# Weight splits inside other phases, decay factors at the start, the flag read in the last batch, and a landing buffer of its own

## The chip, the cores and the metric

The kernel runs on one core of a Trainium2 chip. The metric is the device time of one execution in microseconds (us); lower is better. Engines are called by their names in the profile: PE (TensorE matmul, with PEld its weight load), DVE (VectorE), ACT (ScalarE), POOL (GpSimd) and SP (SyncE, which here only issues DMAs; its queue is SPq).

## The reference

x has the shape 8 x 1024 x 256 (8 batches of 1024 tokens with 256 features). Four layers follow each other, each on the layernorm of x and added to x:

```python
x = x + attention(layernorm(x))          # 2 heads of 128, partial rope, causal softmax
x = x + ffn(layernorm(x))                # silu(x Wg) * (x Wu) @ Wd; int32 weights * 1/127, hidden 768
x = x + linear_attention(layernorm(x))   # 8 heads of 64, decay sigmoid(decay_log) per step, sigmoid gate
x = x + ffn(layernorm(x))                # the same weights again
```

The linear attention is a scan over the tokens: S = g S + k v^T, z = g z + k, out = (q S) / (q z + eps), with q and k being elu(.) + 1.

## The kernel before

x stays in SBUF as tensor X (64 tiles of 128 tokens x 256). Four phases run one after the other, each a block of five instruction streams that wait for each other by semaphores, with all engines meeting between phases: attention (8 batches), ff1, linear attention (8 batches in 16 halves of 512 tokens), ff2. A feed-forward phase works in 16 units of 512 tokens. To get precision from fp32r matmuls, an operand is split into a high part (a copy rounded to fp32r) and a low part (value minus high part), and two or three products are summed.

The feed-forward unit (lines 817 to 1071) is where most of what follows happens. In unit u each engine runs f = 0 to 5 over the hidden columns, 128 at a time, in this order:

- PE: gate(f) and up(f) (line 1026, 4 matmuls each), then down(f - 3) (line 1037, 16 matmuls). gate(f) waits for silu(f - 3), up(f) for h(f - 3), and down for both parts of h. The unit begins when both parts of its normalised, transposed input are there (pe_wait).
- ACT: silu(f) (L951), then the high part of h(f - 1) (L941). At f = 4, ahead of silu(4), it makes the high part of the input of unit u + 1 (act_high, L271), which waits for that input to have landed.
- DVE: h(f) (L990), then the low part of h(f - 1) (low_part, L974); in addition statistics of unit u + 2 at f = 0 and 1, the residual of unit u - 1 at f = 2 (L981), the normalisation of unit u + 2 at f = 3 (L156), and at f = 4 the 32 x 32 block transposes of unit u + 2 (dve_blocks, L255), which wait until the input of unit u + 1 has landed, as both pass through one buffer (ln_xn).
- POOL: 1/sqrt(var) for unit u + 2 (L167, L170), then the low part of the input of unit u + 1 (pool_low, L276).
- SP: 16 DMAs of 32 KB that put the transposed blocks of unit u + 1 in place (sp_move, L266). It waits for up(5) of unit u - 1, since the blocks land where that unit's low part lay (ln_xl, ff_odd_xl), and for the blocks.

The splits of weights stand where they are needed. The feed-forward weights (4608 columns of int32) are cast by POOL in the last attention batch (L465), their low part is taken in three pieces by DVE (L654) and squared in three pieces by ACT (L555) at steps 9, 10 and 11 of that batch; the sum says whether any low part is nonzero, and PE reads that flag (low_any) as a register at the begin of ff1 and ff2 and chooses between two and four products. At the begin of ff1 ACT copies the low weights (L933); at the begin of ff2 ACT casts the weights anew (L936) and DVE takes the low part (L968). At the begin of the linear phase ACT and DVE and POOL split its weights (L1225 to L1227, L1293, L1206, L1209), while decay factors are made from 12 columns by a chain DVE, ACT (Exp, Ln), DVE, ACT (Exp) (L1288 to L1303); PE waits for each part.

## Time and profile before

| what | before |
| --- | --- |
| median of 3 runs | 1981.17 us (1980.4 to 1982.3) |
| the profiled execution | 1982.85 us, its span 1981.1 us |
| PE busy | 1891.3 us (95%) |
| DVE busy | 1367.3 us (69%) |
| ACT busy | 889.7 us (45%) |
| POOL busy | 451.7 us (23%) |
| first matmul of attention, ff1, linear, ff2 | 13.72, 564.71, 853.80, 1698.05 us |
| ff1 units 1 to 14, ff2 units 1 to 14 | 244.48 us, 243.66 us |
| mean granted PE clock | 0.994 |

A timeline row gives the start in us from the span's begin, the duration in us, the engine, the line of the kernel, the instruction with its output and inputs and their shape, and in brackets how long the engine had been idle before it and who ended that. PE's matmuls overlap in these rows, so the distance of their starts is their pace. The granted clock is 1.00 at 2.4 GHz and 0.50 at 1.2 GHz.

### The profile page before, as it was taken

How to read it: one execution, taken by the hardware profiler on the slowest of the kernel's cores; microseconds unless marked ns; L12 is line 12 of the kernel's file. 1: busy time of each engine (PE TensorE's matmuls, PEld its weight loads, DVE VectorE, ACT ScalarE, POOL GpSimd, SP SyncE). 2: the span in 40 equal slices, each digit the busy share in tenths (PEclk: the TensorE clock that was granted, in tenths of full speed). 3: DMA queues.
4: the chain of work that ended last, by engine and by line, in shares of the span. 5: the costliest groups of instructions: out<-in, count | busy, mean ns of one | idle time of the engine just before them, and what ended most of it. 6: DMA issues, size and time to landing. Idle time of an engine off the chain costs nothing. (4 is left out here: it accounts for less than half of the span.)

```text
span 1981.1 us, 36996 instructions
## 1 busy us (share of the span) xinstructions
PE 1891.3 (95%) x12419; PEld 1639.4 (83%) x12419; DVE 1367.3 (69%) x3222; ACT 889.7 (45%) x1708; POOL 451.7 (23%) x362
## 2 busy tenths in 40 slices
PE   6999999999989999969999999999999998899998
PEld 5888888888778888858888888888888887788887
DVE  6666566656667888756766667766666677778885
ACT  5555556655654444453333333333333332444443
POOL 2112201220312222132222222222222222221220
PEclk9999999999999999989999999999999999999999
DMA  6100000000021111110000000000000000122222
GB/s 217 58 1 0 0 0 0 0 0 0 12 75 30 30 30 30 32 53 11 12 12 12 11 11 11 11 11 11 11 11 11 11 12 12 32 64 63 53 61 58
DMA packets 230887, 53.23 MB, mean 27 GB/s; under 512 B 209952, under 2 KB 229024, under 8 KB 230432
## 3 DMA queue, kind: packets, MB, share of 16 engines
q1 hardware_dynamic: 229696, 49.54, 11.7%
q10 hardware_dynamic: 1120, 2.75, 0.4%
q8 instruction: 43, 0.70, 0.2%
q14 instruction: 28, 0.23, 0.0%
HBM read 18.69 MB, written 8.39 MB: 14 GB/s over the span
## 5 line engine op out<-in xcount | busy, mean ns | idle before, releaser
L990 DVE SCALAR_TENSOR_TENSOR ff_h<-PS,ff_silu 128x512 f32<-128x512 f32 x192 | 130.9, 682 | 121.9 <-PE PS L1026 53.2
L951 ACT ACTIVATE ff_silu<-PS 128x512 f32<-128x512 f32 x192 | 114.0, 595 | 199.7 <-PE PS L1026 199.7
L1214 POOL TENSOR_TENSOR lin_yg_lo<-stage,lin_yg_hi 128x512 fp32r<-128x512 f32 x64 | 82.0, 1281 | 504.5 <-ACT lin_yg_hi L1248 504.5
L1037 PE MATMUL PS<-ff_w_hi,ff_h_hi 128*128 128x256 f32 x768 | 191.3, 282 | 2.1 <-ACT ff_h_hi L941 1.4
L1037 PE MATMUL PS<-ff_w_hi,ff_h_lo 128*128 128x256 f32 x768 | 191.9, 283 | 0.0
L318 PE MATMUL PS<-ln_xh,lin_w_hi 128*128 128x512 f32 x384 | 153.4, 400 | 15.6 <-DVE lin_w_lo L1293 8.6
L974 DVE TENSOR_TENSOR ff_h_lo<-ff_h,ff_h_hi 128x512 fp32r<-128x512 f32 x192 | 164.2, 855 | 0.2
L1026 PE MATMUL PS<-ln_xh,ff_w_hi 128*128 128x512 f32 x384 | 152.0, 396 | 11.6 <-issue 4.5
L730 PE MATMUL PS<-probT,v_a 128*128 128x128 f32 x1152 | 154.0, 279 | 4.3 <-DVE oT_lo L589 4.3
L1324 DVE TENSOR_TENSOR lin_AD<-PS,lin_decay 128x512 f32<-128x512 f32 x128 | 82.2, 684 | 109.9 <-PE PS L1470 109.9
L1037 PEld LDWEIGHTS PS<-ff_w_hi,ff_h_hi 128*128 128x128 f32 x768 | 145.6, 190 | 13.7 <-issue 2.9
L1026 PE MATMUL PS<-ff_odd_xh,ff_w_hi 128*128 128x512 f32 x384 | 151.8, 395 | 5.2 <-issue 2.4
L730 PEld LDWEIGHTS PS<-probT,v_a 128*128 128x128 f32 x1152 | 138.9, 192 | 19.5 <-issue 12.9
L318 PE MATMUL PS<-ln_xh,lin_w_lo 128*128 128x512 f32 x384 | 151.3, 394 | 0.0
L1037 PEld LDWEIGHTS PS<-ff_w_hi,ff_h_lo 128*128 128x128 f32 x768 | 146.3, 190 | 6.0
L318 PE MATMUL PS<-ln_xl,lin_w_hi 128*128 128x512 f32 x384 | 151.0, 393 | 0.0
L1026 PE MATMUL PS<-ff_odd_xl,ff_w_hi 128*128 128x512 f32 x384 | 150.8, 393 | 0.0
L1026 PE MATMUL PS<-ln_xl,ff_w_hi 128*128 128x512 f32 x384 | 150.6, 392 | 0.0
L702 PE MATMUL PS<-qk 128*128 128x512 f32 (+3 forms) x384 | 144.7, 488 | 0.0
L594 DVE TENSOR_REDUCE neg_max<-PS 128x1 f32<-128x256 f32 (+7 forms) x128 | 96.6, 755 | 65.5 <-PE PS L705 64.3
L455 POOL TENSOR_TENSOR qk<-qk,swapped 64x512 f32<-64x512 f32 x64 | 81.9, 1280 | 256.1 <-DVE swapped L584 254.2
L271 ACT ACTIVATE ln_xh<-ln_xl 128x1024 fp32r<-128x1024 f32 x32 | 33.9, 1060 | 232.2 <-DMA ln_xl<-ln_xn 232.2
(159 smaller groups left out, 4893.1 us busy)
## 6 DMA issues: line engine op xcount, KB each, us to landing
ln_xl<-ln_xn SPq DMA_DIRECT2D x512, 32.0 KB, 2.0
X<-in_x SPq DMA_DIRECT2D x8, 1024.0 KB, 5.3
ff_odd_xl<-ln_xn SPq DMA_DIRECT2D x256, 32.0 KB, 2.0
out_x<-X SPq DMA_DIRECT2D x16, 512.0 KB, 2.9
stage<-in_w_lin SPq DMA_DIRECT2D x1, 2048.0 KB, 8.2
stage<-in_w_gate SPq DMA_DIRECT2D x2, 768.0 KB, 4.3
stage<-in_w_up SPq DMA_DIRECT2D x2, 768.0 KB, 5.8
stage<-in_w_down SPq DMA_DIRECT2D x2, 768.0 KB, 7.5
```

The costliest lines, as they stand in the source:

```text
L318: last = nc.tensor.matmul(out, w, x, start=n == 0, stop=n == len(terms) - 1)
L455: done = nc.gpsimd.tensor_tensor(qk[rows, s, h, at], qk[rows, s, h, at], swapped[rows, 2 * half + s, :], ALU.add)
L594: nc.vector.tensor_reduce(neg_max[:, n:n + 1], score_rows(n), AX.X, ALU.max, negate=True).then_inc(max_done.sem, 1)
L702: last = nc.tensor.matmul(bank[:, 0:w], qk[:, 0, h, i * P:(i + 1) * P], qk[:, 1, h, c:c + w], start=True, stop=not diag)
L730: last = nc.tensor.matmul(O, V[:, j, h * DA:(h + 1) * DA], probT[:, n % 2, j, :], start=j == 0, stop=j == i)
L951: nc.scalar.activation(silu[:, f % NB_GU, :], PS[:, f % NB_GU, :], ACT.Silu, scale=W_SCALE).then_inc(silu_done.sem, 1)
L974: nc.vector.tensor_tensor(h_lo[:, slot(par, f), :], h[:, f % 2, :], h_hi[:, slot(par, f), :].bitcast(F32), ALU.subtract).then_inc(lo_done. ...
L990: nc.vector.scalar_tensor_tensor(h[:, f % 2, :], PS[:, NB_GU + f % NB_GU, :], W_SCALE, silu[:, f % NB_GU, :], ALU.mult, ALU.mult).then_inc ...
L1026: ins = nc.tensor.matmul(PS[:, bank, :], w, x, start=n == 0, stop=n == len(parts) - 1)
L1037: ins = nc.tensor.matmul(Y[:, t // 2, (t % 2) * M:(t % 2 + 1) * M], a[:, slot(par, f), t * P:(t + 1) * P], w[:, f % NF, :], start=f == 0 a ...
L1214: nc.gpsimd.tensor_tensor(yg_lo[:], yg, yg_hi[:].bitcast(F32), ALU.subtract).then_inc(yg_lo_done.sem, 1)
L1324: nc.vector.tensor_tensor(AD[:, c % 2, r], PS[:, r, :].rearrange("p (j t) -> p j t", t=P), D[:].rearrange("p (j r) t -> p r j t", r=2)[:, ...
```

## The change

- In attention the feed-forward weights are loaded right after batch 1 of x. In batch 0 POOL casts them in place to floats, copies them to the high part and subtracts it (4608 columns each time); ACT squares the low part in 9 pieces of 512 columns at steps 7 to 15 of that batch. The flag is summed, transposed and reduced in the first part of the last batch, and PE reads it there once.
- The decay factors of the linear phase that don't depend on the table `dist` are made at the very begin, on ACT ahead of the attention weights and on DVE ahead of the first statistics; their inputs come as one DMA.
- In a feed-forward phase the moved blocks land in a tensor of their own (`raw`). SP waits for the low part of unit u to be made rather than for up(5) of unit u - 1. ACT makes the high part of unit u + 1 at f = 3 instead of f = 4, after waiting for up(5) of unit u - 1.
- In ff1 ACT and POOL split the linear weights in 8 pieces of 512 columns, one at the end of each of units 5 to 12. SP loads these weights in unit 1. POOL copies the low feed-forward weights at the begin of ff1.
- In the linear phase POOL splits the output weights, the tables that need `dist` are made by ACT ahead of the gate items of the first half, and POOL casts the feed-forward weights to floats at the end of batch 0.
- At the begin of ff2 POOL makes the high part in 13 pieces and the low part in two (3072 and 1536 columns), with the statistics and the low part of unit 1's input between them.
- Loops are unrolled further: SP runs units 1 and 2, and ACT's and POOL's streams run units 1 to 4, ahead of the loop.

```diff
-    def sp_move(self, sp, unit, par):
+    def landing(self, par, raw):
+        return self.raw[:] if raw else self.parts[par][1][:].bitcast(F32)
+    def sp_move(self, sp, unit, par, raw=False):
         wait_alone(sp, self.blocks_done.sem, self.blocks_done.at(unit, 1), self.sp_passed)
-        lo = self.parts[par][1][:].bitcast(F32)
+        lo = self.landing(par, raw)
...
+def act_decays(nc, act, env):
+    act.wait_ge(prep, 2)
+    nc.scalar.activation(tmp_b, tmp_a, ACT.Exp, scale=-1.0).then_inc(prep_act, 1)
+    act.wait_ge(prep_act, 1)
+    nc.scalar.activation(tmp_a, tmp_b, ACT.Ln, bias=1.0).then_inc(prep_act, 1)
+    act.wait_ge(prep, 5)
+    nc.scalar.activation(env["lin_decay_c"][:], log_g[:, HB:], ACT.Exp, scale=float(P)).then_inc(prep_act, 1)
...
                     pool.wait_ge(rotated.sem, rotated.at(b, 2 * NHALF))
+                    if first:
+                        pool.wait_ge(env["ff_loaded"], 16 * NLOAD)
+                        raw = env["stage"][:, 0:NW]
+                        nc.gpsimd.tensor_copy(raw, raw.bitcast(I32)).then_inc(env["ff_high"], 1)
+                        pool.wait_ge(env["ff_high"], 1)
+                        nc.gpsimd.tensor_copy(env["ff_w_hi"][:], raw).then_inc(env["ff_high"], 1)
+                        pool.wait_ge(env["ff_high"], 2)
+                        nc.gpsimd.tensor_tensor(raw, raw, env["ff_w_hi"][:].bitcast(F32),
+                                                ALU.subtract).then_inc(env["ff_low"], 1)
...
-                        if last and n in SPLIT_STEPS:
-                            part = SPLIT_STEPS.index(n)
-                            act.wait_ge(env["ff_low"], part + 1)
+                        if first and n >= NS - NPART:
+                            part = n - (NS - NPART)
+                            act.wait_ge(env["ff_low"], 1)
...
+                dve_decays(nc, dve, env)
                 dve.wait_ge(x_loaded, 16)
                 ln.dve_stats(dve, 0)
...
+                    if last:
+                        pe.wait_ge(env["low_done"], 1)
+                        env["wide"] = pe.value_load(env["low_any"][:].bitcast(I32))
...
-                        if not first:
+                        if left:
+                            if not first:
+                                wait_alone(sp, front.lo_done.sem, front.lo_done.at(u, 1), front.sp_passed)
+                        else:
                             wait_alone(sp, up_ready.sem, up_ready.at(u - 1, NF), front.sp_passed)
-                        nfront.sp_move(sp, nu, npar)
+                        nfront.sp_move(sp, nu, npar, raw=bool(left))
...
-                        if f == NF - 2 and upcoming:
+                        if f == (NF - 3 if left else NF - 2) and upcoming:
                             nfront, nu, npar = upcoming
-                            nfront.act_high(act, nu, npar)
+                            if left and not first:
+                                act.wait_ge(up_ready.sem, up_ready.at(u - 1, NF))
+                            nfront.act_high(act, nu, npar, raw=bool(left))
...
+                    if first and nth == 2:
+                        low_weights(slice(0, 2 * KT * FF))
                     if upcoming:
                         nfront, nu, npar = upcoming
-                        nfront.pool_low(pool, nu, npar)
+                        nfront.pool_low(pool, nu, npar, raw=bool(left))
+                    if first and nth == 2:
+                        low_weights(slice(2 * KT * FF, NW))
...
+                def lin_high(n):
+                    at = bass.ds(n * LIN_PIECE, LIN_PIECE)
+                    act.wait_ge(env["lin_loaded"], 32)
+                    nc.scalar.activation(lin_flat(env["lin_w_hi"])[:, at], stage[:, at], ACT.Copy).then_inc(env["lin_hi"], 1)
...
-                for j in range(NP):
-                    dve.wait_ge(prep_hi, j + 1)
-                    nc.vector.tensor_tensor(qk_cols(w_lo, j), qk_cols(raw, j), qk_cols(w_hi, j).bitcast(F32),
-                                            ALU.subtract).then_inc(prep_lo, 1)
...
+                            if first and half == 0 and it == 2 * NP:
+                                decay_tables()
```

## Rows read from the trace of the kernel before

**Rows 1.** The page's first part: busy time of each engine.

```profile
PE 1891.3 (95%) x12419; PEld 1639.4 (83%) x12419; DVE 1367.3 (69%) x3222; ACT 889.7 (45%) x1708; POOL 451.7 (23%) x362
```

**Rows 2.** Timeline, PE in ff1: gate(4), gate(5) of unit 4, start of unit 6.

```profile
645.19 0.40 PE L1026 MATMUL PS<-ln_xh,ff_w_hi 128*128 128x512 f32 x1
...
647.99 0.40 PE L1026 MATMUL PS<-ln_xh,ff_w_hi 128*128 128x512 f32 x1
...
668.25 0.49 PE L1026 MATMUL PS<-ln_xh,ff_w_hi 128*128 128x512 f32 x1 [0.18 <-POOL ln_xl L276]
```

**Rows 3.** Timeline of one loop unit in ff1: SP, ACT, POOL and DVE.

```profile
652.61 10.48 SPq L266 DMA_DIRECT2D ln_xl<-ln_xn  x16
...
664.46 1.06 ACT L271 ACTIVATE ln_xh<-ln_xl 128x1024 fp32r<-128x1024 f32 x1 [2.68 <-DMA ln_xl<-ln_xn]
665.42 0.58 ACT L951 ACTIVATE ff_silu<-PS 128x512 f32<-128x512 f32 x1
...
665.60 2.41 POOL L276 TENSOR_TENSOR ln_xl<-ln_xl,ln_xh 128x1024 fp32r<-128x1024 f32 x1 [6.25 <-ACT ln_xh L271]
...
666.09 0.70 DVE L990 SCALAR_TENSOR_TENSOR ff_h<-PS,ff_silu 128x512 f32<-128x512 f32 x1 [1.93 <-issue]
666.70 1.85 DVE L974 TENSOR_TENSOR ff_h_lo<-ff_h,ff_h_hi 128x512 fp32r<-128x512 f32 x1
668.48 1.23 DVE L255 STREAM_TRANSPOSE ln_xn<-ln_xn 128x1024 f32<-128x1024 f32 x1
```

**Rows 4.** Timeline, DVE at f = 3 of the same unit.

```profile
661.58 0.69 DVE L990 SCALAR_TENSOR_TENSOR ff_h<-PS,ff_silu 128x512 f32<-128x512 f32 x1 [0.38 <-PE PS L1026]
662.19 0.68 DVE L974 TENSOR_TENSOR ff_h_lo<-ff_h,ff_h_hi 128x512 fp32r<-128x512 f32 x1
662.79 1.38 DVE L156 TENSOR_SCALAR ln_xn<-X,ln_mean_var,ln_rstd 128x256 f32 x4
```

**Rows 5.** Timeline, SP's moves just after the loop, and at the begin of ff2.

```profile
789.88 11.28 SPq L266 DMA_DIRECT2D ln_xl<-ln_xn  x16
...
1696.22 10.41 SPq L266 DMA_DIRECT2D ff_odd_xl<-ln_xn  x16
```

**Rows 6.** By line and form: the long POOL operations, and DVE beside one of them.

```profile
L1293 DVE TENSOR_TENSOR lin_w_lo<-stage,lin_w_hi x4: 678/1777/5060, 852.9 to 861.2; 128x512 fp32r<-128x512 f32 x4
...
L1206 POOL TENSOR_TENSOR lin_w_lo<-stage,lin_w_hi 128x2048 fp32r<-128x2048 f32 x1 | 5.1, 5095 | 1.8 <-ACT lin_w_hi L1226 1.8
L465 POOL CAST ff_w_hi<-stage 128x4608 fp32r<-128x4608 int32 x1 | 4.0, 4032 | 0.1
...
L1203 POOL MEMSET lin_v<- 128x2080 f32 x1 | 1.8, 1831 | 0.0
...
L1202 POOL MEMSET lin_state<- 128x520 f32 x1 | 0.5, 531 | 7.5 <-POOLq L881 7.5
```

**Rows 7.** Timeline, begin of the kernel (DVE, ACT), and the logarithm before the linear phase.

```profile
4.51 1.28 ACT L487 ACT_TABLE_LOAD   x1 [4.51 <-issue]
6.39 2.71 DVE L132 BATCH_NORM_STATS2 ln_stats<-X 128x6 f32<-128x256 f32 x8 [6.39 <-DMA X<-in_x]
...
856.58 0.21 ACT L1232 ACTIVATE lin_tmp_a<-lin_tmp_b 128x12 f32<-128x12 f32 x1
```

**Rows 8.** Timeline, batch 0: end of POOL's rope additions, and ACT's exp of step 9.

```profile
34.27 2.62 POOL L455 TENSOR_TENSOR qk<-qk,swapped 64x512 f32<-64x512 f32 x2 [0.63 <-DVE swapped L584]
...
52.92 0.79 ACT L496 ACTIVATE prob<-PS,neg_max 128x640 f32<-128x640 f32 x1 [0.73 <-DVE neg_max L594]
```

**Rows 9.** Waits of PE over the whole span: us in total, times, longest us.

```profile
PE PS L720 <- ACT probT L506: 4.9, 3, 1.8
```

**Rows 10.** PE's two waits at the begin of the linear phase; stretch after the first.

```profile
853.80 0.77 PE L318 MATMUL PS<-ln_xh,lin_w_hi 128*128 128x512 f32 x1 [8.27 <-DVE lin_w_lo L1293]
...
868.67 0.77 PE L318 MATMUL PS<-ln_xh,lin_w_hi 128*128 128x512 f32 x1 [7.04 <-DVE lin_qT L1314]
...
854.00:856.00 2.00, 2.00 (x5) 1.59 (x6) 2.00 (x1) 1.97 (x3) 2.00 (x1) 0.50 0.00 0
```

More of the change, by code:

```diff
@@ L45 @@
 NW = 2 * KT * FF + NF * M
-NPART = 3
+NPART = 9
+NLOAD = 3
 WPART = NW // NPART
@@ L754, in turn @@
                                 out_projection(b, -1)
+                            if m == 0 and last:
+                                pe.wait_ge(env["low_summed"], 1)
+                                nc.tensor.transpose(low_row, env["low_sum"][:], ident[:]).then_inc(env["low_transposed"], 1)
                     values(b, 0)
@@ L779, in turn @@
                     if last:
-                        pe.wait_ge(env["ff_squares"], NPART)
-                        for part in range(NPART):
-                            ins = nc.tensor.transpose(PS[0:1, 4, part * P:(part + 1) * P],
-                                                      env["low_squares"][:, part:part + 1], ident[:])
-                        ins.then_inc(env["low_transposed"], 1)
                         out_projection(b, NS - 1)
@@ L852, in feed_forward_phase, with run_units @@
         out_v = io["out"].rearrange("b (n p) m -> p (b n) m", p=P)
-        def run_units(eng, unit):
+        def run_units(eng, unit, pairs_before=0, on_pair=None):
             unit(0, 0, True, 2)
-            with eng.Fori(0, NU // 2 - 2) as p:
+            for p in range(pairs_before):
                 unit(p * 2 + 1, 1, False, 2)
                 unit(p * 2 + 2, 0, False, 2)
+            with eng.Fori(0, NU // 2 - 2 - pairs_before) as p:
+                for k in range(2):
+                    unit(p * 2 + (2 * pairs_before + 1 + k), 1 - k, False, 2)
+                    if on_pair:
+                        on_pair(p * 2 + k)
             unit(NU - 3, 1, False, 2)
@@ L985, in unit @@
                     after = after_next(u, left)
+                    if first:
+                        after[0].ln.dve_stats(dve, after[1])
                     for f in range(NF):
@@ L996, in unit @@
                         if after:
-                            if f == 0:
+                            if f == 0 and not first:
                                 after[0].ln.dve_tile_stats(dve, after[1], range(UT))
-                            if f == 1:
+                            if f == 1 and not first:
                                 after[0].ln.dve_aggregate(dve, after[1])
@@ L1013, in _, with wait_weights @@
                 open_signals(pe, gate_ready, up_ready, down_done)
-                pe.wait_ge(env["low_done"], 1)
-                wide = pe.value_load(env["low_any"][:].bitcast(I32))
-                def wait_weights(parts):
-                    if not split_before:
-                        pe.wait_ge(prep_hi, parts)
+                wide = env["wide"]
+                def wait_weights(pieces):
+                    if nth == 2:
+                        pe.wait_ge(prep_hi, pieces)
                 def gate_or_up(sxu, bank, hi, lo, f, terms, done):
@@ L1058, in unit @@
                                 pe.wait_ge(x_done.sem, x_done.at(u, 0))
+                            if first and f == LAG:
+                                wait_weights(2 * NF + 1)
+                                if terms == 4:
+                                    pe.wait_ge(prep_lo, 2)
                             if f >= LAG or not first:
@@ L1184, in turn @@
                             gated_low(b, UT * half - 1)
+                        if first and half == 0:
+                            pool.wait_ge(decays, 1)
                         for j in range(NP):
@@ L1198, in turn @@
                                 nfront.pool_low(pool, n, 0)
+                        if first and half == NHALF - 1:
+                            ff_float()
                     if last:
@@ L1254, in turn @@
                                 gated_high(b, UT * half - 1)
+                            if first and half == 0 and it == 2 * NP:
+                                decay_tables()
+                            if first and half == 0 and it == 3 * NP:
+                                act.wait_ge(zeroed, 2)
                             m = NITEM * half + it
@@ L1387, in turn @@
                         nln.dve_aggregate(dve, nturn)
+                        if first and half == 0:
+                            dve.wait_ge(decays, 2)
+                            nc.vector.tensor_tensor(D[:], D[:], dist[:, 1, :].unsqueeze(1).to_broadcast([P, HB, P]),
+                                                    ALU.mult).then_inc(masked, 1)
+                            dve.wait_ge(masked, 1)
+                            dve.wait_ge(zeroed, 2)
                         decayed_scores(b, c0, 0)
@@ L1529, in turn @@
                         for it in range(NITEM):
-                            if half == 0 and first and it < 2 * NP:
-                                pe.wait_ge(prep_lo, it // 2 + 1)
+                            if half == 0 and first and it == 0:
+                                pe.wait_ge(env["lin_lo"], LIN_PIECES)
                             if half == 0 and first and it == 2 * NP:
```

226 lines of the change are left out of this document (114 added, 112 removed).

## The prediction

> **What bounds the kernel now.** I read the page's busy times first: PE has matmuls under way for 1891.3 of 1981.1 us [rows 1], so work moved off its neighbours can give back no more than PE's waits. Then the list of PE's waits, which names them: the begin, 15 us before the linear phase [rows 10], 4.9 us in the last attention batch [rows 9], some microseconds at the other phase borders. Last the timeline of one loop unit of the feed-forward phases, since half the change acts there and 28 units share it. PE's own pace is 647.99 - 645.19 = 2.80 us for one f [rows 2], six of which are 16.8 us. The unit takes 17.2, and each starts 0.24 us after POOL has made the low part of its input (668.25 against 665.60 + 2.41) [rows 2, 3]. What makes POOL late is a ring that runs once per unit [rows 3]. SP issues the 16 moves from 652.61; ACT, idle 2.68 us for the landing, starts the high part 11.85 us later, at 664.46, and behind it in its queue come silu(4) at 665.42, then on DVE h(4) at 666.09, the low part of h(3) at 666.70 and the block transposes, which end at 669.71. SP's next moves start 0.1 us after those, as its first of these did after theirs. Landing to transposes is 669.71 - 664.46 = 5.25 us, and 11.85 + 5.25 + 0.1 = 17.2 us: the ring is the period, PE has 0.4 us to spare in each unit. The transposes, not up(5) of unit u - 1, release SP. In it the low part takes 1.85 us instead of 0.68 [rows 3, 4]: it has two SBUF inputs and ends 0.5 us behind POOL's subtraction.
>
> **The feed-forward phases.** The own landing buffer takes away SP's wait for up(5) of unit u - 1; by the above that wait isn't the last, so it gives 0. SP's new wait, for the low part of unit u, isn't the last either: POOL ends that at 668.01, the transposes at 669.71; the moves queued behind it lose nothing. But ACT's high part moves from f = 4 to f = 3. It still waits for the landing, and now silu(3) is queued behind it. DVE must pass from there through h(3), the low part of h(2), the normalisation, h(4) and the low part of h(3) before the transposes. Three operations join the ring: h is 0.61 us to the next start (662.19 - 661.58), the low part 0.60 (662.79 - 662.19), the normalisation 1.38 less the 0.09 by which neighbours overlap, 1.29 [rows 4]. That is 2.5 us, and the unit takes 17.2 + 2.5 = 19.7 us, against 16.8 of PE work. PE will wait near the end of each unit, at down(2), for the low part of h(2), which DVE makes 4.1 us after ACT's high part starts. Both phases have 14 such units: 28 x 2.5 = 70 us. Could the ring be shorter? If the low part weren't held, by 1.2 us; but POOL's subtraction starts 1.1 us after ACT's and lasts 2.4, and DVE's low part comes 2.2 after it, so it is held as now. So 1.3 to 2.5 per unit, 36 to 70 us; I take 2.5, since its terms are rows of these same instructions. Unit 0 adds some 1.4 us in each phase by the same shift, of which the earlier first matmul (below) hides 0.6 at most in ff1: 2 us for both. Code that SP runs for the first time makes the 16 moves 0.8 us longer (11.28 against 10.48) [rows 3, 5]; SP unrolls one pair more, so two more units of each phase pay it: 3 us.
>
> In unit 0 of ff2 POOL now makes all weight parts. A copy costs 0.1 us and 0.83 ns a column (from 531 ns at 520 and 1831 at 2080 columns) [rows 6], by which the 12 pieces of 256 cost 0.3 to 0.4 each and the last 1.4, 6 us together; PE takes 0.9 us per piece and isn't held up. After 1.3 us for 1/sqrt(var), the subtraction of 3072 columns at 2.4 to 2.5 ns (5.09 us at 2048) lasts 7.4 us. What such an operation does to DVE is seen at L1293: 678 ns alone, 5060 beside the 5095 ns of L1206 [rows 6]. So the low part of h(2) waits till about 15 us into the block, unit 1's input low part follows till 17.1 (its SP moves start as before, 1696.22 [rows 5]), and the second subtraction, 3.7 us, holds DVE again in unit 1. Bounds: 0 if DVE's two-input work falls between, 11 if all of both is paid; the slack of two f between a low part and its down hides most, and I take 3. In ff1 POOL's copy of 4608 columns ends before DVE has h(0): 0. Pieces of the linear weights: ACT 0.6 us and POOL 1.3 us at the end of 8 units, outside the ring: 0, or 8 x 0.6 = 5 if in it.
>
> The Trainium skill, "SBUF — State Buffer", section "SBUF: two separate sides", calls the shared port pair an exclusive lock, held by the one that starts first for the whole instruction. By that rule DVE is shut out for all 7.4 us of the new subtraction; if POOL's operations of more than the traced 5.1 us gave way in between, the 3 us above would be 0. The rule agrees with L1293's row and speaks against the move of weight work to POOL.
>
> Sum for both phases: 70 + 2 + 3 + 3 = +78 us (range 40 to 86).
>
> **The begin.** DVE makes the decay factors ahead of its first statistics, which start at 6.39 us when x lands [rows 7]. ACT's queue gets one more DMA, some 0.45 us, so its table load starts at 5.0; load 1.28, Exp 0.21, load 1.28, Ln 0.21 and gaps are 3.0 us, 8.0; three small DVE operations 0.6 us; the statistics start at 8.7, 2.3 us late. From there to the first projection DVE is the chain. +2.3 us (0 to 4, the end where the small DMA lands late). The skill's page "ScalarE: Activation LUTs", section "Table sets: the hidden batching unit", lists a set that has both exp and ln: by it one load would do and the delay would be 1.0. In the trace the logarithm of L1232 has a load of its own, as the exponentials on both sides of it; I go by that.
>
> **Batch 0.** POOL's rope additions end at 36.89 [rows 8]. Then two copies of 4608 columns at 4.03 (the cast) and a subtraction of 4608 at 2.4 to 2.5 ns, 11.2 us, end at 56.4. ACT reaches its first square ahead of the exp of step 9, which began at 52.92 after 0.73 of idle time; now it begins after 56.4 + 0.8 for the square, 4.4 us late. What is queued behind ACT's wait is this exp and the transposed probabilities of step 8, and PE waits for both. PE has some 1.5 to 2 us in hand there: +3 us (0.5 to 4.4). The other eight squares of 0.8 us fit into ACT's idle time.
>
> **The last batch.** DVE's three subtractions, ACT's three squares and the three waits of PE that they cause go: -4.9 us [rows 9]. PE reads the flag there, 0 to 1.2 us; I take 0.7. -4.2 us. The first matmul of ff1 comes about 1 us earlier, which is worth 0, as SP's moves and the ring begin with the block.
>
> **The linear phase.** PE's waits of 8.27 and 7.04 us [rows 10] end with weights that are ready. Entering the block costs about 3.4 of the first, which stays: -4.9 and -7.0. After the first the clock was granted at 0.50 (854 to 856) [rows 10]; if both were followed by one such stretch of 7 to 10 us, PE did some 9 us of work at half pace: up to -4.5 more. ACT's tables are 12 exponentials of 0.3 us, 3.6 us, ahead of the gate items; PE has four banks of projections, the scores and key transposes to do meanwhile: 0 to 2. The 3.4 us stop may still cost one stretch at 0.50, 0 to 3.4. I take -14 us (-17 to -8). POOL's cast at the end of batch 0 (4.0 us) lies between two low parts that are a unit of work apart: 0 to 2, I take 0. The earlier first matmul of ff2 is again swallowed by the ring.
>
> **Sum.** 78 + 2.3 + 3 - 4.2 - 14 = +65 us on the profiled execution's 1982.85: 2048. The median of the runs stands 1.7 below that execution, so I forecast 2046 us.
>
> **Rivals.** (1) Faster: the early high part does open the ring. If blocks land before ACT is through with silu(2), at about 8 us of the unit, ACT never waits, POOL is done 4 us before the next unit, and PE runs at 16.8 us: 28 x 0.4 = 11 us gained, 3 us more from the early first matmuls, the slow moves of code run for the first time (0.9 us in 8 units, 7 us) vanish as well. With -4.2, -14 and +5 that is 1982.85 - 34 = 1949 us. The point is the time of the landing: the moves take 11.9 us from the transposes, so these would have to end 4 us ahead of the unit's start, while in rows 3 they end 1.5 us after it. Against it also: the ring contains every operation named above whatever the start. 9%. (2) The 17.2 us ring stays as it is, since DVE's three operations were done in time it idles anyway (1.93 us ahead of h(4) [rows 3]): 1982.85 - 13 = 1970 us. Against it: that idle time is the wait for this very landing. 4%. (3) The clock: PE now stops some 2.9 us in every unit. If that brings stretches at 0.50 as after the stops of rows 10, a unit loses a few tenths to 2 us more: 2060 to 2100 us. For it: the long stop was followed by 0.50; against: busy 85% of each unit. 7%. The forecast: 80%.
>
> **How the numbers follow.** Own range of the forecast, from the bounds (36 to 78 for the ring, 10 for the borders): 2028 to 2062. Leaving out (1) and most of (2), the range is 2012 to 2064. A difference of 0.2%, 4 us, is what a measurement of this kernel can tell. Faster is (1) and (2), 13%; within 0.2% 2%; slower 85%.
>
> **What would show it.** Unit starts 19.7 us apart; DVE's idle time ahead of h(3), ACT's high part still waiting for the DMA; a new line in PE's waits, L1037's down on the low part of h, nearly 3 us, 28 times; SP's moves starting 0.1 us after the transposes. In the linear phase the waits of 8.27 and 7.04 us gone. I am wrong if ACT's high part shows no wait for the DMA, or if units start 17 us apart.

## The result, and the profile after

The changed kernel takes 2049.21 us (median of 4 runs, 2047.61 to 2058.03), the kernel before in the same comparison 1981.74 us (1980.4 to 1982.81). The ratio is 1.035, 95% interval 1.032 to 1.038: 67.5 us slower, where 2046 us had been forecast. The profiled execution of the changed kernel is the slowest of the four, 2058.03 us with a span of 2056.3 us, and also has the lowest mean granted clock, 0.981; the other three have 0.985 or 0.986. The stages below are those of this execution, so they add up to 75.2 us, not 67.5.

Busy times and the chain of work from the page of the changed kernel, answering to [rows 1]:

```profile
PE 1925.2 (94%) x12417; PEld 1656.4 (81%) x12417; DVE 1350.0 (66%) x3213; ACT 879.3 (43%) x1716; POOL 504.6 (25%) x389
...
SPq 5%; PE 4%; DVE 3%; issue 2%; DMA 1%; ACT 0%; DVEq 0%; ACTq 0%
```

The kernel before had PE alone at the head of that chain (PE 12%). Now SP's issues come first (5%), with PE at 4% and DVE at 3%. PE's work is the same; its busy time is 33.9 us longer, since more of its matmuls ran under a clock of 0.50, and since those of the linear halves are slower (4.5 us, below).

PE's waits (us in total, times, longest us):

```profile
PE PS L1117 <- DVE ff_h_lo L1053: 59.8, 28, 3.8
PE PS L201 <- DVE ln_xn L157: 15.9, 1, 15.9
...
PE PS L324 <- DVEq L76: 5.4, 1, 5.4
...
PE PS L761 <- ACT probT L551: 1.9, 1, 1.9
```

The first line is new: 28 waits of a down matmul for the low part of h, 2.1 us on average. They stand in 26 of the 28 loop units and in unit 0 of each phase; in units 3 PE, slowed by a stretch of 6.8 us at clock 0.50, came after the low part. The two waits of [rows 10] and the 4.9 us of [rows 9] are gone; 5.4 us are left at the entry of the linear phase. The 1.9 us on transposed probabilities lie in batch 0.

One loop unit of ff1 (timeline: start, us, engine, line, operation, idle time before it and its releaser), answering to [rows 3, 4]. L277 is the high part of the input, L282 its low part, L1071 h, L1053 the low part of h, L257 the block transposes, L272 SP's moves:

```profile
677.20 1.06 ACT L277 ACTIVATE ln_xh<-ff_raw 128x1024 fp32r<-128x1024 f32 x1 [5.14 <-DMA ff_raw<-ln_xn]
678.16 0.58 ACT L1031 ACTIVATE ff_silu<-PS 128x512 f32<-128x512 f32 x1
...
678.34 2.39 POOL L282 TENSOR_TENSOR ln_xl<-ff_raw,ln_xh 128x1024 fp32r<-128x1024 f32 x1 [6.15 <-ACT ln_xh L277]
...
678.83 0.69 DVE L1071 SCALAR_TENSOR_TENSOR ff_h<-PS,ff_silu 128x512 f32<-128x512 f32 x1 [4.55 <-ACT ff_silu L1031]
679.44 1.84 DVE L1053 TENSOR_TENSOR ff_h_lo<-ff_h,ff_h_hi 128x512 fp32r<-128x512 f32 x1
681.20 1.37 DVE L157 TENSOR_SCALAR ln_xn<-X,ln_mean_var,ln_rstd 128x256 f32 x4
...
681.42 0.36 PE L1117 MATMUL PS<-ff_w_hi,ff_h_hi 128*128 128x256 f32 x1 [1.22 <-DVE ff_h_lo L1053]
...
682.50 0.68 DVE L1071 SCALAR_TENSOR_TENSOR ff_h<-PS,ff_silu 128x512 f32<-128x512 f32 x1
683.10 0.67 DVE L1053 TENSOR_TENSOR ff_h_lo<-ff_h,ff_h_hi 128x512 fp32r<-128x512 f32 x1
683.70 1.23 DVE L257 STREAM_TRANSPOSE ln_xn<-ln_xn 128x1024 f32<-128x1024 f32 x1
...
685.02 1.89 SPq L272 DMA_DIRECT2D ff_raw<-ln_xn  x3
```

ACT stands 5.14 us for the landing, ahead of silu(3). DVE idles 4.55 us for that silu and then has h(3), a held low part of h(2), the normalisation, h(4), the low part of h(3) and the transposes to do: from ACT's start to their end 684.93 - 677.20 = 7.73 us, where it was 5.25 before. SP starts 0.1 us later. PE stood from 680.20 to 681.42 for the low part of h(2) in this unit.

### The profile page after: what moved, and what is told of

The parts are those of the page before. It is cut to its first block and busy times, and to the rows that moved or that the text cites. A ratio compares the mean times of both kernels' runs of the same rounds, so it can differ in the third digit from the quotient of the medians.

```text
span 2056.3 us, 36946 instructions
## 1 busy us (share of the span) xinstructions
PE 1925.2 (94%) x12417; PEld 1656.4 (81%) x12417; DVE 1350.0 (66%) x3213; ACT 879.3 (43%) x1716; POOL 504.6 (25%) x389
## 5 line engine op out<-in xcount | busy, mean ns | idle before, releaser
L1071 DVE SCALAR_TENSOR_TENSOR ff_h<-PS,ff_silu 128x512 f32<-128x512 f32 x192 | 130.4, 679 | 201.2 <-ACT ff_silu L1031 140.9
L1117 PE MATMUL PS<-ff_w_hi,ff_h_hi 128*128 128x256 f32 x768 | 201.1, 293 | 63.9 <-DVE ff_h_lo L1053 59.8
L1117 PEld LDWEIGHTS PS<-ff_w_hi,ff_h_hi 128*128 128x128 f32 x768 | 150.3, 196 | 88.2 <-issue 70.6
L1117 PE MATMUL PS<-ff_w_hi,ff_h_lo 128*128 128x256 f32 x768 | 198.4, 290 | 0.0
L1053 DVE TENSOR_TENSOR ff_h_lo<-ff_h,ff_h_hi 128x512 fp32r<-128x512 f32 x192 | 167.6, 873 | 0.2
L1019 ACT ACTIVATE ff_h_hi<-ff_h 128x512 fp32r<-128x512 f32 x192 | 120.3, 627 | 99.0 <-DVE ff_h L1071 98.9
L1106 PE MATMUL PS<-ln_xh,ff_w_hi 128*128 128x512 f32 x384 | 156.5, 407 | 3.2 <-POOL ff_w_hi L994 1.6
L1106 PE MATMUL PS<-ff_odd_xh,ff_w_hi 128*128 128x512 f32 x384 | 156.0, 406 | 1.1 <-POOL ff_odd_xl L282 1.1
L1106 PE MATMUL PS<-ff_odd_xl,ff_w_hi 128*128 128x512 f32 x384 | 155.6, 405 | 0.0
L1117 PEld LDWEIGHTS PS<-ff_w_hi,ff_h_lo 128*128 128x128 f32 x768 | 151.2, 197 | 5.3
L1106 PE MATMUL PS<-ln_xl,ff_w_hi 128*128 128x512 f32 x384 | 154.8, 403 | 0.0
```

Of the source, the lines that this page charges most:

```text
L1019: nc.scalar.activation(h_hi[:, slot(par, f), :], h[:, f % 2, :], ACT.Copy).then_inc(hi_done.sem, 1)
L1053: nc.vector.tensor_tensor(h_lo[:, slot(par, f), :], h[:, f % 2, :], h_hi[:, slot(par, f), :].bitcast(F32), ALU.subtract).then_inc(lo_done. ...
L1071: nc.vector.scalar_tensor_tensor(h[:, f % 2, :], PS[:, NB_GU + f % NB_GU, :], W_SCALE, silu[:, f % NB_GU, :], ALU.mult, ALU.mult).then_inc ...
L1106: ins = nc.tensor.matmul(PS[:, bank, :], w, x, start=n == 0, stop=n == len(parts) - 1)
L1117: ins = nc.tensor.matmul(Y[:, t // 2, (t % 2) * M:(t % 2 + 1) * M], a[:, slot(par, f), t * P:(t + 1) * P], w[:, f % NF, :], start=f == 0 a ...
```

## Where the time went, stage by stage

Each stage runs from the first matmul of one part to the first matmul of the next, by their starts in the timeline. The letters are the experiments of the next section: A high part back at f = 4, C kernel before with the transposes at f = 3, E four edits, I best version.

| stage, us | before | after | A | C | E | I |
| --- | --- | --- | --- | --- | --- | --- |
| begin to first projection | 18.76 | 20.89 | 20.87 | 18.89 | 18.84 | 19.48 |
| batch 0, to the first transposed probabilities | 14.89 | 16.39 | 14.96 | 16.48 | 14.96 | 17.15 |
| rest of batch 0 | 52.01 | 55.78 | 54.04 | 52.01 | 52.17 | 52.18 |
| batches 1 to 6 | 403.60 | 403.94 | 403.78 | 403.33 | 403.70 | 403.41 |
| last batch | 75.45 | 70.15 | 70.16 | 75.53 | 70.24 | 70.26 |
| ff1 unit 0 | 15.09 | 16.37 | 14.88 | 15.00 | 15.63 | 15.51 |
| ff1 units 1 to 14 | 244.48 | 278.23 | 242.23 | 235.09 | 235.47 | 234.72 |
| ff1 unit 15 and linear half 0 | 88.83 | 77.45 | 75.83 | 86.09 | 74.05 | 73.09 |
| linear halves 1 to 14 | 714.97 | 719.94 | 719.72 | 714.65 | 721.44 | 714.60 |
| linear half 15 | 69.97 | 69.49 | 68.24 | 69.41 | 69.72 | 71.47 |
| ff2 units 0 and 1 | 32.73 | 41.36 | 39.69 | 32.65 | 40.01 | 32.54 |
| ff2 units 2 to 14 | 225.67 | 258.24 | 224.61 | 217.96 | 218.67 | 218.31 |
| ff2 unit 15 to the end | 24.65 | 28.07 | 24.59 | 26.1 | 24.5 | 26.7 |

After less before: 79.6 us in the two feed-forward phases, +2.1 at the begin, +5.3 in batch 0, -5.3 in the last batch, -11.4 around the entry of the linear phase, +5.0 in its halves, the rest -0.1. Of the 5.3 us in batch 0, 1.5 are not the change's: the stretch up to the first transposed probabilities takes 14.9 us where the granted clock rises to 1.00 by 18.9 us (before, A, E, H) and 16.4 to 17.2 where it rises at 22 to 25 us (all others, among them B, C, J and K, whose attention is that of the kernel before).

## Experiments

### A and B: the place of ACT's high part, taken back and done alone

A is the changed kernel with one line back:

```diff
-                        if f == (NF - 3 if left else NF - 2) and upcoming:
+                        if f == NF - 2 and upcoming:
```

> The changed kernel with one edit: ACT makes the high part of unit u+1's input at f = 4 again, as before the change; landing buffer, SP's wait, unrolling and all weight work stay. The ring theory: three DVE operations (h, low part, normalisation, 2.5 us) leave the ring, units 1 to 14 come 17.0 to 17.2 us apart instead of 19.5, PE's 28 waits of 2 to 3 us at down(2) for the low part of h go, and with them most stretches at granted clock 0.50. 28 x 2.35 = 66 us and some 10 us of clock: 1968 to 1984 us. Rival 1, the new landing buffer with SP's wait for POOL's low part sets the period: units stay above 19 us, 2035 to 2050 us. Rival 2, half and half: units of 18 to 18.5 us, about 2010 us.

Measured: 1979.21 us (10 runs), ratio to before 0.9988 (0.9978 to 0.9997). B is the kernel before with the reverse edit and nothing else:

```diff
-                        if f == NF - 2 and upcoming:
+                        if f == (NF - 3 if left else NF - 2) and upcoming:
```

> The kernel before with one edit: ACT makes the high part of unit u+1's input at f = 3 instead of f = 4, nothing else. The ring theory: units 1 to 14 go from 17.2-17.5 to 19.5 us in both feed-forward phases, 28 waits of PE at down for the low part of h of 2 to 3 us, 2042 to 2060 us (the upper end with stretches at clock 0.50 after these stops). Rival, the slower units of the changed kernel come from its landing buffer or SP's wait: no change, 1977 to 1985 us.

Measured: 2053.65 us (4 runs), ratio 1.0364 (1.0348 to 1.038), 72.3 us slower. PE's waits of B, the kernel before with that one line:

```profile
PE PS L1037 <- DVE ff_h_lo L974: 62.0, 30, 3.7
```

The ring in A (timeline): the same rows as above, with neither h(3) nor the normalisation between the high part and the transposes.

```profile
694.12 1.38 DVE L157 TENSOR_SCALAR ln_xn<-X,ln_mean_var,ln_rstd 128x256 f32 x4
...
695.72 1.06 ACT L277 ACTIVATE ln_xh<-ff_raw 128x1024 fp32r<-128x1024 f32 x1 [2.60 <-DMA ff_raw<-ln_xn]
...
697.96 1.86 DVE L1053 TENSOR_TENSOR ff_h_lo<-ff_h,ff_h_hi 128x512 fp32r<-128x512 f32 x1
699.74 1.23 DVE L257 STREAM_TRANSPOSE ln_xn<-ln_xn 128x1024 f32<-128x1024 f32 x1
```

High part to end of the transposes is 700.97 - 695.72 = 5.25 us, the period of the transposes 17.1 us. In the changed kernel the period is 19.57. A still has the landing buffer, SP's wait for POOL's low part, the longer unrolling and all moved weight work, and its ring is that of the kernel before to 0.1 us: none of these sets the period. One line of the change is the whole loss, and both rivals of A fall.

### C and D: opening the ring

If the ring is real, it can be opened at its other end. C is the kernel before, with the block transposes right behind the normalisation:

```diff
                             if f == 3:
                                 after[0].ln.dve_normalise(dve, after[1])
-                            if f == 4:
                                 after[0].dve_blocks(dve, after[1], (front, u + 1))
```

> The kernel before with one edit: DVE makes the block transposes of unit u+2 at f = 3 right behind the normalisation, instead of at f = 4; ACT's high part stays at f = 4. The ring theory: from landing to transposes no silu, h or low part is left, so the ring is about 11.85 + 1.3 = 13.2 us and no longer sets the period; PE's own pace of 16.8 us does: 0.3 to 0.6 us less in 28 units, 1963 to 1973 us. Rival 1, the ring isn't what bounds the unit of the kernel before but PE itself with POOL's low part: no change, 1979 to 1984. Rival 2, DVE stands at the transposes for the landing and holds back h(4): units of 17.5 to 18.5 us, 1990 to 2015.

Measured: 1962.22 us (5 runs), ratio 0.9908 (0.9894 to 0.9923), 19 us faster and a little below the expected range. Two starts of units in C (timeline, PE), without a wait ahead of them:

```profile
698.96 0.40 PE L1025 MATMUL PS<-ln_xh,ff_w_hi 128*128 128x512 f32 x1
...
715.73 0.40 PE L1025 MATMUL PS<-ff_odd_xh,ff_w_hi 128*128 128x512 f32 x1
```

715.73 - 698.96 = 16.77 us, the same from unit 2 of ff1 and from unit 1 of ff2 on: PE's own pace (unit 1 of ff1 takes 17.12 us). The kernel before needed 17.1 to 17.2 in the loop and 18 in the units where SP ran new code; with the ring open the slow moves cost nothing either, and this is the part of the gain that the expectation left out. The transposes now have slack, as ACT's rows of C show, where the high part meets a landing that is nearly there:

```profile
710.17 1.06 ACT L271 ACTIVATE ff_odd_xh<-ff_odd_xl 128x1024 fp32r<-128x1024 f32 x1 [0.58 <-DMA ff_odd_xl<-ln_xn]
```

D is the same edit in the changed kernel, high part still at f = 3. It tests the arithmetic of the ring, since only h(4) and one low part leave it.

> The changed kernel with one edit: block transposes at f = 3 right behind the normalisation; ACT's high part stays at f = 3 too. The ring theory by its terms: silu(4), h(4) and the low part of h(3) leave the ring (h and low part 0.61 + 0.60 us), so 19.5 - 1.2 = 18.3 us a unit (18.1 to 18.6), 28 x 1.2 = 34 us less and some microseconds of clock: 2005 to 2020 us. Rival, only the place of the high part matters: no change, 2045 to 2055. Rival 2, the whole ring opens: 17 us a unit, 1970 to 1980.

Measured: 2024.33 us (4 runs), ratio 1.0212 (1.0196 to 1.0227). The transposes end 6.79 us after the high part's start instead of 7.73, and units take 18.65 us: 0.92 less, not 1.2. The rest is in one row of D:

```profile
676.88 1.25 DVE L257 STREAM_TRANSPOSE ln_xn<-ln_xn 128x1024 f32<-128x1024 f32 x1 [0.15 <-DVE ln_xn L157]
```

Right behind the normalisation, whose output they read, the transposes wait for its end and 0.15 us more, while DVE operations that don't depend on each other overlap by some 0.07. So this edge between two dependent operations costs some 0.2 us that the sum of durations hasn't. The mechanism stands, its time was a little over the expected range.

### E: begin and batch 0

E is the changed kernel with A's and C's edits and two more:

```diff
-NPART = 9
+NPART = 6
...
                 ln.dve_stats(dve, 0)
+                dve_decays_end(nc, dve, env)
                 ln.dve_normalise(dve, 0)
...
                 nc.scalar.activation(wqkv_hi[:, :, nq:], wqkv_raw[:, :, nq:], ACT.Copy).then_inc(prep_hi, 1)
+                act_decays_end(nc, act, env)
```

The two functions hold what stood in the decay chains behind the logarithm; DVE does its part in the gap in which POOL makes 1/sqrt(var).

> The changed kernel with four edits that act in different stages: the high part at f = 4, the block transposes at f = 3, ACT's squares in 6 pieces of 768 columns at steps 10 to 15 of batch 0, and the second halves of the decay chain moved (DVE's behind its first statistics, ACT's behind the first two weight copies). By stages: units of 16.8 us as PE's pace in ff1 and in ff2 from unit 2 on; the first projection at 18.8 to 19.0 us again instead of 20.9; batch 0 66.9 to 67.1 us as before the change instead of 69.0 in the run with the high part at f = 4; ff2's units 0 and 1 still 3 to 7 us longer than PE's work, since POOL's two subtractions shut DVE out. In all 1947 to 1958 us. Rival: if the low part of the input comes late for another reason than the ring, units stay at 17.1 and the time is 1960 to 1968.

Measured: 1963.84 us (4 runs), ratio 0.9911 (0.9894 to 0.9927), so 6 us above the expected range. The first projection is back at 18.84 us, so the decay chain had cost 2.0. The rest of batch 0 is back at 52.17 us from 54.04: ACT's wait ahead of the first square had cost 1.9 us. It is this row of the changed kernel:

```profile
58.83 0.63 ACT L600 ACTIVATE swapped<-stage 128x512 f32<-128x512 f32 x1 [3.00 <-POOL stage L504]
```

Units run at 16.8 us. What is above the range lies in two stages: ff2 units 0 and 1 (40.01 us, where C takes 32.65) and the linear halves (721.44, where C takes 714.65).

### F and G: the begin of ff2

F is E without POOL's two subtractions at the begin of ff2:

```diff
-                    if first and nth == 2:
-                        low_weights(slice(0, 2 * KT * FF))
...
-                    if first and nth == 2:
-                        low_weights(slice(2 * KT * FF, NW))
```

> As the run of the four edits, but POOL's two subtractions at the begin of ff2 (3072 and 1536 columns, the low part of the weights, which the two-product path doesn't read) are left out of the computation. If the shared-port stall of DVE behind them is what makes ff2's units 0 and 1 long, both units return to 15 to 17 us and the time falls by 3 to 7 us. If the long units come from POOL's 13 copies or from SP's moves, it falls by less than 1 us.

Measured: 1957.06 us (4 runs), 6.8 us below E. That is within the 3 to 7 us expected. Units 0 and 1 take 14.64 and 16.86 us, together 8.5 less than in E, and that is above the 3 to 7 us by which these units were expected to be long. The rows of E show how the stall comes about, POOL first, then DVE (L1067 is the low part of h there):

```profile
1682.68 7.36 POOL L1013 TENSOR_TENSOR ff_w_lo<-stage,ff_w_hi 128x3072 fp32r<-128x3072 f32 x1
1690.01 2.81 POOL L282 TENSOR_TENSOR ff_odd_xl<-ff_raw,ff_odd_xh 128x1024 fp32r<-128x1024 f32 x1
1692.77 3.52 POOL L1013 TENSOR_TENSOR ff_w_lo<-stage,ff_w_hi 128x1536 fp32r<-128x1536 f32 x1
...
1684.54 6.05 DVE L1067 TENSOR_TENSOR ff_h_lo<-ff_h,ff_h_hi 128x512 fp32r<-128x512 f32 x1
1690.51 6.57 DVE L157 TENSOR_SCALAR ln_xn<-X,ln_mean_var,ln_rstd 128x256 f32<-128x256 f32 x4
1697.12 1.25 DVE L257 STREAM_TRANSPOSE ln_xn<-ln_xn 128x1024 f32<-128x1024 f32 x1
```

The low part ends 0.55 us after POOL's first subtraction. Then the normalisation, which has one SBUF tensor as input and takes 1.37 us alone, lasts 6.57 us beside the other two. DVE does three pieces of work in 13.8 us. PE waits three times in these two units of E, 1.24, 1.14 and 2.96 us, and its clock is granted at 0.50 for two stretches of 3.4 us (from 1693.0 and from 1699.9), which cost it up to 3.4 us more.

The normalisation consists of four operations. Two of them are held: they take 2.45 and 3.56 us, until some 0.15 us after the end of POOL's subtraction beside them, and the other two 0.40 each. The kernel before had such a case in unit 0 of ff1, DVE's row and then POOL's (timeline; [rows 4] has the same normalisation alone, 1.38 us):

```profile
575.85 3.47 DVE L156 TENSOR_SCALAR ln_xn<-X,ln_mean_var,ln_rstd 128x256 f32<-128x256 f32 x4
...
576.43 2.42 POOL L276 TENSOR_TENSOR ff_odd_xl<-ff_odd_xl,ff_odd_xh 128x1024 fp32r<-128x1024 f32 x1 [1.02 <-ACT ff_odd_xh L271]
```

G gives the weights of ff2 back to ACT (3 copies) and DVE (3 subtractions), as in the kernel before:

```diff
+                if nth == 2:
+                    act.wait_ge(env["ff_float"], 1)
+                    for at in parts_of_w:
+                        nc.scalar.activation(w_hi[:, at], stage[:, at], ACT.Copy).then_inc(prep_hi, 1)
...
+                if nth == 2:
+                    for n, at in enumerate(parts_of_w):
+                        dve.wait_ge(prep_hi, n + 1)
+                        nc.vector.tensor_tensor(w_lo[:, at], stage[:, at], w_hi[:, at].bitcast(F32),
+                                                ALU.subtract).then_inc(prep_lo, 1)
```

> As the run of the four edits, but ff2's weights are split as before the change: ACT makes the high part in 3 copies and DVE the low part in 3 subtractions at the begin of the block, POOL has none of it. PE waits about 1.5 to 3 us at the first two gates and DVE starts 5 us late, as in the kernel before; units 1 to 15 at 16.8 us. Ends 1 to 4 us below the run of the four edits: 1944 to 1955 us. If the begin costs as much as POOL's stall did, the two are equal.

Measured: 1958.21 us (4 runs), ratio 0.9875 (0.9858 to 0.9891), 5.6 us below E where 1 to 4 were expected, and 3 us above the range, since E itself was above its own; units 0 and 1 take 32.64 us. Moving this step to the idle engine was worth less than leaving it where it was.

### H, J and K: why the linear halves take 0.36 us more

Nobody had touched the matmuls of the linear halves, and PE waits for the same things there. The windows of halves 1 to 14 (us, PE busy, clock, DMA share, GB/s) of the changed kernel, then of the kernel before:

```profile
939.20:1659.14 719.94, 711.46 (x5099) 1.00 0.07 11
```

```profile
913.11:1628.08 714.97, 706.97 (x5099) 1.00 0.07 11
```

The clock is full in both; the same 5099 matmuls are under way 4.5 us longer. What differs by the diff is where tensors lie. The new small tensors stand between the layernorm's tensors and the weights, and the linear weights lie at the upper end of SBUF. The distances that follow are counted from the sizes and the order of the tensors in the kernels; no trace shows addresses. In the kernel before, the high part of the input (ln_xh) and every weight of the three kinds of phase lie a multiple of 1024 bytes apart within a partition; in the changed kernel the linear weights lie 896 bytes more than such a multiple from it, in E, F and G 928 more, and the weights of attention and feed-forward 384 more. Three kernels move tensors in the kernel before and change nothing else:

```diff
         env["norm"] = NormBuffers(nc, ctx)
+        pad = sb("pad", [P, 80])
```

> The kernel before with 320 unused bytes of SBUF per partition between the layernorm's tensors and all that lie behind them, nothing else. It asks why the changed kernel's linear halves take 0.36 us more and its attention batches 0.06 more though their instructions are the same and PE's waits too: there the matmuls of the projections come 0.2325 us apart instead of 0.227. If the distance in SBUF between a matmul's two operands does it, this kernel's batches (67.27 us) or halves (51.47 and 50.65 us) change by 0.05 to 0.5 us each, 1 to 7 us in all. If not, they stay within 0.02 us and the time is 1977 to 1984 us; then the extra traffic or the order of the engines in the changed kernel is the cause.

> The kernel before with the same 320 unused bytes, but ahead of the layernorm's tensors instead of behind them: the inputs of all projections and all weights move together, their distance stays a multiple of 1024 bytes. If the distance between weights and input sets the pace of the matmuls, the halves stay at 714.97 us for 14 and the time is 1979 to 1984. If absolute addresses do, or the distance to X or stage, the halves take 720 to 721 and the time is 1986 to 1991, as with the bytes behind them.

> The kernel before with 256 unused bytes behind the layernorm's tensors instead of 320. If distances that are a multiple of 256 bytes are as good as those of 1024: 715 us for the 14 halves, 1979 to 1984 us. If not: 720 to 721 us and 1986 to 1991 us as with 320.

Measured: 320 bytes behind the layernorm's tensors (H) 1988.98 us (5 runs), ratio 1.0038 (1.0024 to 1.0052). The same bytes ahead of them (J) 1980.19 us (10 runs), ratio 1.0001 (0.999 to 1.0012). 256 bytes behind them (K) 1981.5 us (10 runs), ratio 0.9998 (0.9989 to 1.0007). The windows of halves 1 to 14 of H, J and K, in this order:

```profile
910.83:1631.63 720.80, 712.97 (x5098) 1.00 0.07 11
```

```profile
910.94:1625.75 714.81, 706.38 (x5099) 1.00 0.07 11
```

```profile
913.05:1627.92 714.87, 706.53 (x5099) 1.00 0.07 11
```

Some of the projections' matmuls of 512 columns in the same 50.7 us of both, one half in the kernel before and about one in H (by line and form: count, busy us, mean ns), H first, then the kernel before:

```profile
L318 PE MATMUL PS<-ln_xl,lin_w_hi 128*128 128x512 f32 x24 | 9.5, 396 | 0.0
```

```profile
L318 PE MATMUL PS<-ln_xl,lin_w_hi 128*128 128x512 f32 x24 | 9.3, 389 | 0.0
```

Moving both by the same bytes changes nothing (J), moving them apart by 320 does (H), and 256 bytes are harmless (K). So the 5 us are the price of the place of the weights; I, below, gets them back. H shifts all that lies behind the layernorm's tensors; that it is the distance between a matmul's two operands, and not that between ln_xh and some other tensor, is likely, since these matmuls are what slows, but no run moved one tensor alone.

### I: all of it together

I is G, with the small decay tensors ahead of the layernorm's and 32 unused bytes, so that the distances are multiples of 1024 bytes in attention and feed-forward, and such a multiple plus 512 for the linear weights:

```diff
-        env["norm"] = NormBuffers(nc, ctx)
         for n, cols in (("lin_const", HB + NP + 1 + NP), ("lin_log_g", HB + NP), ("lin_tmp_a", HB + NP), ("lin_tmp_b", HB + NP),
                         ("lin_decay_k", HB), ("lin_decay_c", NP), ("lin_bias", NP)):
             env[n] = sb(n, [P, cols])
+        pad = sb("pad", [P, 8])
+        env["norm"] = NormBuffers(nc, ctx)
```

> As the run with ff2's weights on ACT and DVE, but the small decay tensors lie ahead of the layernorm's in SBUF, with 32 unused bytes: all weights of attention and feed-forward lie a multiple of 1024 bytes from the high part of the input again, as in the kernel before, and the linear weights 512 bytes more than such a multiple (864 to 928 bytes more until now). If the distance between the two operands sets the pace and 512 will do, linear halves 1 to 14 take 715 instead of 721.4 us, units 1 to 14 of ff1 235.1 instead of 235.5, attention batches 1 to 6 403.5 instead of 403.7: 1950 to 1953 us. If it has to be 1024, the linear halves stay at 720 to 721.5 and the time is 1956 to 1959. If placement has nothing to do with it: 1957 to 1959 with nothing changed anywhere.

Measured: 1947.77 us (5 runs), ratio 0.9828 (0.9815 to 0.9841), 10.4 us below G, more than the distance was expected to bring. The halves are at 714.60 us, 6.8 less than in G, and ff1's units at 234.72, 0.7 less. The rest of the step between the two medians isn't explained by a stage that the edit touches. This version keeps what the change was right about and is 33 us faster than the kernel before (1980.99 us in the same comparison), 101 us faster than the changed one.

## Why the prediction was right, point by point

- **The ring and its 2.5 us.** Right. 17.1 us became 19.57; B alone gives 72.3 us where 70 were forecast. PE waits at down(2) for the low part of h(2), 28 times, as forecast, though for 2.1 us on average where nearly 3 were named. The low part stayed held (1.84 us), so the lower value of 1.3 us a unit was rightly not taken.
- **Buffer and SP's wait at 0.** Right (A).
- **Unit 0 and SP's new code, 2 + 3 us.** In B the two units 0 are 0.75 and 0.47 us longer than before, 1.2 where 2 were taken; unit 0 of ff1 in the changed kernel is 1.28 us longer, but it holds a stretch of 3.4 us at clock 0.50 that neither B nor the kernel before has there. The two ring periods around SP's new code behind ff1's loop were 20.74 and 20.99 us against 19.57, some 1.3 each where 0.8 were taken.
- **ff2's weights on POOL, 3 us (0 to 11).** Mis-sized, within its bounds: 7.4 us with the ring open (40.01 in E, 32.64 in G, which splits them as the kernel before does; F, which leaves the low part out, is 8.5 below E), 6.6 with the ring closed (41.36 us in the changed kernel, 34.78 in B). The durations were right (7.36 us for 3072 columns, where 7.4 were worked out), and so was the hold on the low part of h(2). What was missed is the normalisation. I had counted only "two-input work" as held; two of its four operations, with one SBUF input each, are held too, which makes it 6.57 us instead of 1.37, and they stand in DVE's queue ahead of h. The slack of two f doesn't hide 13.8 us. The trace of the kernel before had a row for it (575.85, above), which the prediction does not use. The Trainium skill, "SBUF — State Buffer", section "SBUF: two separate sides", names DVE operations in a two-port mode beside those with two SBUF inputs, and I had gone by the latter alone. The trace agrees on those with two inputs (the low part, 0.68 us alone, 6.05 here) and shows that one with a single input can be held (0.41 alone, 2.45 and 3.56 here); that it ran in such a mode, no row shows.
- **The begin, 2.3 us.** Measured 2.1, and E gets it back. Exp and ln had separate table loads, 1.28 us each (at 4.90 and 6.43 us in the changed kernel; at 853.76 and 855.29, the second ahead of L1232, in the kernel before), and a third stands ahead of the next exp (7.95).
- **Batch 0, 3 us.** 1.9 to 2.0 us by A and E. In the profiled execution it is 5.3, since the clock rose later (1.5 us) and a stretch of 3.4 us at 0.50 followed PE's stop of 1.9 us (1.7 us, which A doesn't have). POOL's subtraction took 10.0 us where 11.2 were worked out.
- **The last batch, -4.2 us.** Measured -5.3. The wait for the flag was 0.9 us, and PE stood 1.58 us instead of 2.13 ahead of the first matmul of ff1. What made the rest of it, 0.7 us, stays open. I had put an earlier first matmul at nothing, since unit 0 would pay it back; in A it doesn't (14.88 us, 15.09 before).
- **The entry of the linear phase, -14 us (-17 to -8).** Measured -11.4 us, with the ring's longer unit 15 in it; A, whose ring is the old one, has -13.0. The kernels with the old entry (before, B, C, H, J, K) need 86.1 to 88.8 us for ff1's last unit and half 0, those with the new one 73.1 to 77.5.
- **What the prediction left out.** 5.0 us in the linear halves, by the place of the weights. The rows of before can't show it; that the weights move is in the diff.
- **The range.** The bounds as written (40 to 86, 0 to 4, 0.5 to 4.4, -4.9 to -3.7, -17 to -8) give 2000 to 2064 us. The lower ends of 2028 and 2012 don't follow from them; the result lies within all of these.
- **Rival 3, the clock.** Half right. The clock did fall in the feed-forward phases, in some fifteen stretches of 3.4 or 6.8 us, but the price of a few tenths to 2 us a unit was wrong, as the last section shows.

By medians the change costs 67.5 us where 65 were worked out. In the profiled execution, by which the stages are read, it costs 75.2, and the sum was 10 short: 5.0 in the linear halves, 2.6 at their entry, 2.3 in batch 0, 1.6 in the feed-forward phases, less 1.1 in the last batch. That the medians come closer is no merit of the sum: this execution is the slowest of four, and the 5.0 us of the halves stand in no term, so the last 3 us of agreement are in part luck. The term that decided, the ring, was right by itself, as B shows.

## What to carry to other kernels

Before an operation is moved forward in an in-order queue, follow the loop that it belongs to across all engines and units: what counts is not that it can start earlier, but how many operations then stand between a transfer's landing and the issue of the next one. A ring of this kind may be opened at either end; here the useful edit was to move the producer of the transfer (the transposes, 19 us faster), not its consumer (68 us slower). Weight work on an idle engine isn't free if its operations hold those of a busy one, as POOL's subtractions hold DVE's here. New tensors can cost time by moving others: 320 bytes between inputs and weights cost 0.4% here, 256 nothing.

## What the runs showed of the hardware

**The distance between operands.** The projections' fp32r matmuls of 512 columns in the linear phase start 0.228 us apart on average in the kernel before, J, K and I, 0.232 us in H and in the changed kernel and 0.233 in E, F and G (715 us for 14 halves against 720 to 721). So offsets of 0, 256 and 512 bytes beyond a multiple of 1024 were good, 320, 896 and 928 were not. At 384 the gate and up matmuls of the changed kernel start 0.2316 us apart, where the kernel before has 0.2304; where PE sets the pace, that makes ff1's units 1 to 14 235.5 us (E) instead of 235.1 (C). The Trainium skill, "TensorE: Matmul & The Clock Gate", section "Step-by-step: what each phase is for", says that loading the next weights takes no SBUF bandwidth from the running matmul. H, J and K show that there is a small cost which depends on where the operands lie; whether it is that of the two reads meeting, no run here tells.

**A stall of the clock that costs nothing.** PE stops once a unit, and its clock falls to 0.50 for 3.4 us every few units. Windows of ff1's units 6, 7 and 8 of the changed kernel, then two short ones where unit 7 ends and unit 8 begins (us, PE busy, clock, DMA share, GB/s):

```profile
682.45:701.99 19.54, 17.36 (x98) 1.00 0.18 27
701.99:722.38 20.39, 18.07 (x99) 0.95 0.17 26
722.38:741.14 18.76, 17.72 (x98) 0.96 0.19 28
...
722.00:725.40 3.40, 3.40 (x16) 0.74 0.00 0
725.40:728.80 3.40, 3.40 (x22) 1.00 0.35 52
```

Unit 7 is 0.8 us longer and unit 8 0.8 us shorter: 20.39 + 18.76 = 39.15 = 2 x 19.57. The ring runs over SP, ACT and DVE, and its period stays at 19.57 us while PE is slow, since PE has 19.57 - 16.8 = 2.8 us of slack in each unit. The same stretch in a stage that PE bounds is paid in full: the rest of batch 0 took 55.78 us with one of them and 54.04 without (A). In D, where PE stops twice a unit for some 0.9 us each (24.7 us in 26 waits for the high part of h, 23.8 us in 28 for its low part), the mean clock of ff1's units 1 to 14 is 0.99, in the changed kernel, with one longer stop, 0.96:

```profile
PE PS L1116 <- ACT ff_h_hi L1019: 24.7, 26, 4.5
PE PS L1116 <- DVE ff_h_lo L1053: 23.8, 28, 2.3
...
582.30:845.63 263.33, 244.16 (x1345) 0.99 0.22 38
```

**POOL's subtractions hold more than DVE's subtractions.** Beside POOL's low part of the input (2.6 us), the normalisation of C takes 3.47 us instead of 1.38 in every second unit (one of its four operations takes 2.50 us); the slack of the open ring hides it.
